# Transpositions of the probabilities split into two row halves and moved next to the scores, in a fused attention and expert kernel

## The reference, cut to what matters

```python
kv_latent = jnp.einsum('bsd,ld->bsl', x, w_kv_down)
# q from x; k and v from kv_latent; rotary embedding on q and k
scores = jnp.einsum('bhsd,bhtd->bhst', q, k) / jnp.sqrt(jnp.float32(D))
scores = scores + causal[None, None]
probs = jax.nn.softmax(scores.astype(jnp.float32), axis=-1).astype(q.dtype)
out = jnp.einsum('bhst,bhtd->bhsd', probs, v)
...
return jnp.einsum('bsq,dq->bsd', out, wo)
```

## Time and profile before

| what | value |
|---|---|
| median of 3 runs | 302.72 us (302.44 to 302.72) |
| profiled execution, its own time | 303.29 us |
| its span, first to last instruction | 301.5 us |
| busy: PE, PE weight loads, DVE, ACT, POOL | 289.6, 235.0, 229.7, 239.3, 213.5 us |

### The profile page before, as it was taken

The page is one execution under the profiler, slowest core; times in us unless marked ns, Lnnn a source line. Parts: engine busy times, 40 slices in busy tenths (PEclk is TensorE's granted clock), DMA queues, the critical chain, the costliest instruction groups (busy, mean ns, idle before and its releaser), DMA issues.

```text
span 301.5 us, 8603 instructions
## 1 busy us (share of the span) xinstructions
PE 289.6 (96%) x2362; PEld 235.0 (78%) x2362; DVE 229.7 (76%) x909; ACT 239.3 (79%) x863; POOL 213.5 (71%) x325
## 2 busy tenths in 40 slices
PE   8798999999999999999999989999999999999994
PEld 2576888888888888777776779999977778887663
DVE  4889998987777898988898723444377889898981
ACT  4278789898887889989998676677787898999971
POOL 2478878697778669999999982333226899998730
PEclk9999999999999999999999999999999999999999
DMA  6864685879333233444333382000234243543410
GB/s 192 249 133 115 114 276 148 205 194 300 87 75 68 60 75 83 107 101 102 90 97 90 112 245 55 2 0 2 66 93 108 64 113 99 121 106 109 113 37 17
DMA packets 39596, 33.35 MB, mean 111 GB/s; under 512 B 4801, under 2 KB 36674, under 8 KB 39554
## 3 DMA queue, kind: packets, MB, share of 16 engines
q1 hardware_dynamic: 38098, 30.51, 39.8%
q0 software_dynamic: 1024, 2.10, 2.4%
q10 hardware_dynamic: 432, 0.23, 0.3%
HBM read 11.07 MB, written 4.98 MB: 53 GB/s over the span
## 4 chain that ended last, share of the span: by engine, by line
PE 64%; POOL 14%; DVE 9%; issue 6%; DMA 3%; ACT 1%; POOLq 0%; SPq 0%; DVEq 0%; ACTq 0%
PE bank L1199 9%; PE bank L1187 9%; PE bank L1216 8%; PE bank L1450 7%; PE bank L1438 6%; PE bank L1233 6%; POOL probs L499 5%; POOL staged L488 5%; PE bank L1161 3%; DVE rot_out L617 3%; PE bank L1218 3%; PE bank L1189 3%; POOL xn L515 3%; DMA qk_sb<-staged 3%; DVE masked L633 2%
## 5 line engine op out<-in xcount | busy, mean ns | idle before, releaser
L975 ACT ACTIVATE pexp<-masked,negmax 128x128 f32<-128x128 f32 (+1 forms) x256 | 113.9, 452 | 2.2 <-DVE negmax L633 2.2
L499 POOL TENSOR_SCALAR probs<-pexp,rden 128x128 f32<-128x128 f32 (+1 forms) x195 | 84.3, 447 | 27.0 <-DVE rden L640 25.2
L633 DVE CUSTOM_DVE_ANT_0 masked<-bank,mask 128x128 f32<-128x128 f32 (+1 forms) x256 | 75.9, 352 | 21.4 <-PE bank L1189 20.5
L488 POOL TENSOR_TENSOR staged<-rot_out 128x512 f32<-128x512 f32 x56 | 71.4, 1278 | 16.2 <-DVE rot_out L617 15.6
L617 DVE TENSOR_TENSOR rot_out<-bank,rot 128x1024 f32<-128x1024 f32 x64 | 77.7, 1215 | 4.6 <-PE bank L1163 3.5
L997 ACT COPY probsT<-bank 128x384 f32<-128x384 f32 x126 | 54.0, 480 | 27.3 <-PE bank L1199 26.0
L1199 PE MATMUL bank<-ident,probs 128*128 128x128 f32 x384 | 54.0, 275 | 0.7 <-issue 0.5
L975 ACT ACTIVATION_READ_ACCUMULATOR pexp<-masked,negmax 128x1 f32 x256 | 50.0, 195 | 0.0
L1187 PE MATMUL bank<-qk_sb 64*128 64x256 f32 x256 | 47.0, 428 | 1.7 <-DMA qk_sb<-staged 1.3
L1199 PEld LDWEIGHTS bank<-ident,probs 128*128 128x128 f32 x384 | 43.0, 140 | 3.4 <-issue 1.2
L1233 PE MATMUL bank<-vo_sb,ctxT 128*128 128x128 f32 x256 | 37.8, 278 | 0.7 <-ACT ctxT L1004 0.7
(11 more groups left out here) (117 smaller groups left out, 483.6 us busy)
## 6 DMA issues: line engine op xcount, KB each, us to landing
qk_sb<-staged SPq DMA_DIRECT2D x128, 128.0 KB
w_sb<-in_w SPq DMA_DIRECT2D x2, 1024.0 KB, 5.8
w_sb<-in_w SPq DMA_DIRECT2D x4, 512.0 KB, 5.3
sorted_x<-z SPq DMA_DIRECT2D x1, 1408.0 KB, 8.0
sorted_g<-z SPq DMA_DIRECT2D x1, 1152.0 KB, 5.5
out<-res SPq DMA_DIRECT2D x8, 128.0 KB, 2.3
x_sb<-in_x SPq DMA_DIRECT2D x3, 256.0 KB, 3.8
rot<-in_c_rot SPq DMA_DIRECT2D x1, 512.0 KB, 5.7
```

What stands on the lines that cost most here:

```text
L488: pool.tensor_tensor(staged[:, n % 2, :, m % 2, :], rot_out[:, m % 2, :, 0:S], rot_out[:, m % 2, :, S:2 * S], op=ALU.add).then_inc(staged_ ...
L499: pool.tensor_scalar(probs[:, g % 2, i, c], pexp[:, g % 2, i, c], rden[:, g % 2, i, k:k + 1], 1.0, ALU.mult, ALU.mult).then_inc(probs_read ...
L633: t = dve.tensor_tensor_reduce(masked[:, g % 2, i, c], s_bank[i][:, c], mask[:, c], -1.0, -NEG * 1e8, ALU.add, ALU.min, negmax[:, g % 2, i ...
L975: e = act.activation(pexp[:, g % 2, i, c], masked[:, g % 2, i, c], ACT.Exp, bias=negmax[:, g % 2, i, k:k + 1], scale=-1.0, accum_out=rowsu ...
```

## The change

Three things, in slots 2 to 35 and in the periods at 44 to 56:

- `turn` in its new form makes twelve transpositions, two for each block of 128 x 128: one of its 64 rows in partitions 0 to 63, one of those in 64 to 127. The first half goes to `t_bank[0]`, the second to `t_bank[1]`, so a bank holds 64 of each block's 128 query columns, of both heads.
- ACT copies both banks once all twelve are done, each with a strided write that puts its 64 columns of each block in place. Size and number of the copies are as before.
- In slots 2 to 35 `turn(g)` is called at the end of the slot, behind `output` and `values` and ahead of the next slot's scores, and not behind the first projection. In the periods it stays where it was, and only the first turn of a period has the new form.

```diff
+HALVED = (*range(2, G_LEAD - 4), *PERIODS[1:])
+TURN_LAST = range(2, G_LEAD - 4)
...
+        def turned_half(g, i):
+
+            whole = probsT[:, g % 4].rearrange("p i (k q c) -> p (i k) q c", q=2, c=HD)
+            return whole[:, :, i, :]
...
                 if g > 3:
                     act.wait_ge(pv_done, values_through(g - 4))
+                if g in HALVED:
+                    act.wait_ge(probsT_done, 2 * g + 2)
+                    for i in range(2):
+                        act.copy(turned_half(g, i), t_bank[i][:, 0:SW].rearrange("p (n c) -> p n c", c=HD)
+                                 ).then_inc(probsT_ready, 1)
+                    return
...
             def turn(g):
 
+                if g in HALVED:
+                    wait(pe, probsT_ready, 2 * g)
+                    for i in range(2):
+                        for k in range(3):
+                            if k < 2:
+                                pe.wait_ge(probs_ready[i][k], g + 1)
+                            for o, r in zip(t_bank, half_rows):
+                                t = pe.transpose(o[:, (3 * i + k) * HD:(3 * i + k + 1) * HD],
+                                                 probs[r, g % 2, i, k * P:(k + 1) * P], ident[r, r])
+                        t.then_inc(probsT_done, 1)
+                    return
...
                 elif g == G_LEAD + 1:
                     values(g - 1)
-                else:
+                elif g not in TURN_LAST:
                     turn(g)
...
                 if g > 1 and g % 2 == 0 and g - 2 not in ALONE and g not in (G_LEAD, G_LEAD + 2):
                     values(g - 2)
+                if g in TURN_LAST:
+                    turn(g)
                 for m in items(g)[1:]:
                     project(m)
```

## The result

The changed kernel takes 332.08 us (median of 6 runs, 330.87 to 333.35) where the one before takes 302.72: a ratio of 1.0966, 95% interval 1.0946 to 1.0985, slower by 9.7%. The prediction was 323.0 with a range of 314 to 333. The direction and the mechanism hold; the size is 29.4 us where 20.3 were forecast.

The account below looks back on a forecast made before the run. The prediction took PE, busy for 96% of the span, as the bound, with POOL as full in the periods. Its terms +15.8 + 5.8 - 1.3 = +20.3 us on 302.72 gave 323.0 us, range 314 to 333.

Parts of the forecast that it names:

- The loop: Slots 3 to 25: turn, ACT's copies and exponentials, ctxT (2.36 us), output, values, turn again; 4.18 us a slot, +15.8 in all.
- The odd slots from 27 on: Five odd slots of 26 to 35, where the loop also holds: 3.88 us each, +5.8 us together.
- The even ones: Even slots of 26 to 35, set by PE alone: 4.31 us before, -0.27 each, -1.3 us in all.
- The halved turn: Six pairs of half transpositions at 0.062 us: 0.37 us a turn instead of 0.65 on PE.
- the second rival: The loop holds, but a pair costs a full transposition (0.107 us): +8.9 us over 33 slots, 332 us; chance 0.14.
- The first case: The loop as forecast with a turn near 0.37 us: 318 to 329 us; chance 0.63.
- So I take 0.8 of it: Slots 3 to 25: of 9.8 us of other ACT work falling into the loop, 7.8 us lengthens it.
- the small pieces: Slots 3 to 25: 0.5 us for latents waiting for DVE, 0.5 for slot 18, -0.8 for slot 25 without values.
- at a granted clock of 1.00 throughout: Reading of the kernel before, slots 3 to 35 and the periods: TensorE's granted clock was 1.00 throughout.
- the term 0.31: In the loop: 0.31 us from the start of the turn's last matmul to ACT's first probsT copy.
- The periods: Seven periods: 0 us, the middle between -2.0 and +2.1, since POOL fills them as PE does.
- The fourth rival: No wait in front of output, only PE's savings left: -10.2 us, 292.5 us; chance 0.05.

Follow-up runs that it names:

- the added copy: Changed kernel plus one unused 128 x 128 ScalarE copy between the probsT copies in slots 2 to 35: 335.64 us; same copy in the kernel before: 302.99 us.
- The filler: Changed kernel plus ten unneeded matmuls in front of output in odd slots 27 to 35: 327.57 us, ratio 1.0814 to the kernel before.
- the turn-first kernel: Changed kernel with the halved turn behind the scores, ahead of the projection, in slots 2 to 35: 301.12 us; with periods as before, 300.62 us.
- the split-only kernel: Changed kernel with the halved turn left mid-slot, behind the projection and ahead of output, in slots 2 to 35: 304.52 us, ratio 1.0052.

## Why the prediction was right, and where its size was off

- **The loop.** Right in place and size: 4.18 us forecast, 4.17 or 4.18 measured in slots 16, 17 and 20 to 22, and the wait of PE for ctxT in all of them. Moving alone costs 23 us, splitting alone 1.5 to 1.8, and an operation of 0.16 us put into the loop costs 0.16 a slot. (The terms as written add up to 2.35 and 4.16, and not to the recorded 2.36 and 4.18; over 23 slots that is under 0.5 us.) The odd slots from 27 on: 3.88 forecast, 3.89 and 3.88 measured in 29 and 33, but that match is luck, as the last 2.5 us below show. The even ones: 4.31 - 0.27 = 4.04 forecast, 4.01 and 4.02 measured in 30 and 34.
- **The halved turn.** 0.37 us forecast from the logit transpositions at 0.061, 0.36 to 0.37 measured. The bound 0.64, one pair like one full transposition, is excluded, and with it the second rival: the twelve loads span 0.45. The Trainium skill's figure ("TensorE: Matmul & The Clock Gate", section "LDWEIGHTS (loading the stationary operand)"), 107 ns for a load of 128 columns, doesn't hold for these pairs either: they stand 0.062 apart.
- **The range.** 332.08 lies within 314 to 333, but not by what the range was made for. The first case by itself was given 318 to 329 and misses it. The upper end came from the second rival, whose 332 is the number that was measured and whose mechanism, a pair at the price of a full transposition, wasn't there. The next three points are what filled the 9.1 us above 323.0. So the forecast is right in direction and in its main mechanism, and that the range holds the last 3 us is luck.
- **The term that was undersized: ACT's other work in slots 3 to 25.** "So I take 0.8 of it", with the small pieces 8.0 us in all. Measured: 106.44 - 23 x 4.18 = 10.3. Slots 4, 6 and 7 took 4.85, 5.05 and 5.21 us, so +0.67, +0.87 and +1.03. The stage grew by 18.1 where 15.8 were forecast. How the 2.3 us more divide over the pieces of this term no run separates; the added copy shows that all slots of the stage but 18 follow ACT.
- **The term that was missing: the clock.** Slots 26 to 35 were to grow by 5.8 - 1.3 = 4.5 us and grew by 11.5. The filler shows 4.5 of these 7.0 as the clock's: 46.22 against 41.72 with the clock at 1.00. Another 0.8 of it lies in slot 36, behind the stage. The step that failed is "at a granted clock of 1.00 throughout": it was read off the kernel before, in which PE was busy for 99% of these slots. The forecast itself took that away, and yet its sum has no term for the clock.
- **The remaining 2.5 us** are in the term 0.31, the time from the turn's last matmul to ACT's first copy. It holds in slots 3 to 25. In slots 26, 30 and 34 it is 1.36, 0.65 and 0.94 us, though ACT has nothing else to do. The records of ACT in the changed kernel, slot 26, in order of time (start, duration):

```profile
142.55 0.20 ACT L984 ACTIVATION_READ_ACCUMULATOR pexp<-masked,negmax 128x1 f32 x1
144.45 0.86 ACT L1007 COPY probsT<-bank 128x384 f32<-128x384 f32 x2 [1.71 <-PE bank L1216]
```

  The turn's last matmul started at 143.09, so 143.40 was due. Slot 27 then waits 2.59 us for ctxT, which is where the clock falls first. The clock isn't the cause of the hold: with ten fillers and the clock at 1.00 it is 1.35, 0.58, 0.65, 0.64 and 0.92 us in slots 26, 28, 30, 32 and 34, together 2.6 us above 0.31, and the odd slots 29, 31 and 33 that follow take 4.15 to 4.21 us. In the changed kernel only slots 28 and 32, which ran in part at the lower clock, had 0.32, and only behind these two was 3.88 met. With full transpositions moved, the odd slots behind 28, 30 and 32 take 3.69 us each, and the slots behind 26 and 34 take 4.03. So in the first three the hold came only with the halved turns, which stand there behind the values of two slots, and in the other two a part of it is there without them. What holds the copy no row names. It stays open.
- **The periods**: 0 forecast. From slot 42 to the end the changed kernel takes 76.07 us, the one before 75.57; with the periods left as they were, the turn-first kernel was 0.5 us faster, within the intervals. No gain, as argued, and perhaps a small loss.
- **The fourth rival** (no wait in front of output) asked for a ctxT copy within 0.85 us of the first probsT copy; it was 1.64. Moving that copy ahead took PE's wait for ctxT away, but the forecast that only PE's savings would be left was wrong for that kernel too: the same lateness reached the rotations.
- The Trainium skill ("TensorEngine Tiling", section "PSUM Bottleneck") points in the direction that was measured, though the copies didn't become the limit by their duration: ACT's busy time stayed at 75.6 us of these slots. Their place in the order did it.

## What to carry to other kernels

Before work is moved later on one in-order engine, follow the engine that consumes it: everything in its program behind the copy moves too, and the loop back to the first engine can be written down and summed from the trace before anything is built. A chain with 1.3 us of room looked like idle time that costs nothing; adding the same small operation in both kernels (0 against 0.16 us a slot) is a cheap test for whether it still is. If two neighbours in the order are to be joined to save a switch, try the place that makes the work earlier first: here the halved turn behind the slot's scores gave -0.8% in the same slots in which behind the values it gave +9.7%, and -1.2% where it was kept to slots 2 to 23.

## What the runs showed of the hardware

- The granted clock of TensorE fell from 1.00 to 0.50, its lower level of 1.2 GHz, inside a pause of 2.59 us in slot 27, again shortly after one of 1.81 and at the end of one of 2.15. Matmuls without a use, ten in front of output in each odd slot from 27 to 35, held it and made the whole 4.5 us faster. In slots 3 to 25, with pauses of up to 1.45 us, it stayed at 1.00, and so it did with pauses of 1.47 and 1.48 in slots 29 and 33. The Trainium skill ("TensorE: Matmul & The Clock Gate", section "Why this matters for your kernels") warns that idle gaps between stretches of matmuls cost the clock; slot 27 agrees, and with the fillers the lower clock is gone.
- A halved fp32 transposition, 128 columns of weights and 64 moving, runs in pairs 0.062 us apart, where a full one takes 0.107: splitting by rows gives 0.36 us for 0.65 when the split mode is already set. Where it isn't, the two switches of 0.20 eat it: +0.07 us a slot in the split-only kernel.
